# ScalarE writes the normalised tokens of the first pass, gain and bias go into the weights, inputs and statistics run a block ahead

## The reference

```
def _ln(x, g, b):
    m = jnp.mean(x, axis=-1, keepdims=True)
    v = jnp.mean(jnp.square(x - m), axis=-1, keepdims=True)
    return (x - m) * jax.lax.rsqrt(v + EPS) * g + b
h1 = _ln(x, n1_g, n1_b)
x = _attn(h1, h1, q1, k1, v1, o1_w, o1_b, heads) + x
h2 = _ln(x, n2_g, n2_b)
x = _attn(h2, context, q2, k2, v2, o2_w, o2_b, heads) + x
h3 = _ln(x, n3_g, n3_b)
proj = h3 @ ff_w1 + ff_b1
a, g = jnp.split(proj, 2, axis=-1)
return a * jax.nn.gelu(g, approximate=False) @ ff_w2 + ff_b2 + x
```

## Time and profile before

| | |
|---|---|
| median of 3 runs (lowest to highest) | 1429.01 us (1424.47 to 1432.35) |
| time of the profiled execution | 1427.96 us |
| its span, first to last instruction | 1426.1 us |
| mean granted TensorE clock | 0.966 |
| first pass | 0 to 156.1 us of the span |
| T0, T1, T2, T3, T7, end of PE's values | 20.87, 42.67, 57.41, 79.82, 140.54, 152.66 us |
| PE busy over the span | 93% |

### The profile page before, as it was taken

One profiled execution on the slowest core, in us unless ns is written; L12 is line 12 of the kernel. 1 busy time (PEld: TensorE's weight loads), 2 busy tenths in 40 slices (PEclk: granted clock), 3 DMA queues, 4 the chain that ended last, 5 costly groups with the idle time before them and its releaser, 6 DMA issues. The chain is left out here.

```text
span 1426.1 us, 35161 instructions
## 1 busy us (share of the span) xinstructions
PE 1321.4 (93%) x13343; PEld 1228.8 (86%) x13343; DVE 865.8 (61%) x1782; ACT 658.8 (46%) x1521; POOL 369.5 (26%) x468
## 2 busy tenths in 40 slices
PE   3899678999999999999999999999749999999999
PEld 3788667898989989988899899898539999999999
DVE  6776346777777777777777777776355424242421
ACT  2334125565655656656556565565334232323131
POOL 4211312222122122221221212212026342424241
PEclk9999689999999999999999999999759999999999
DMA  4667344444444554554544444442111000000000
GB/s 119 202 195 254 127 120 128 131 150 123 139 143 119 158 154 141 149 157 141 172 126 144 133 133 144 124 123 92 29 41 58 32 29 19 28 18 28 19 5 24
DMA packets 122663, 155.77 MB, mean 109 GB/s; under 512 B 25856, under 2 KB 116368, under 8 KB 122512
## 3 DMA queue, kind: packets, MB, share of 16 engines
q1 hardware_dynamic: 122512, 153.71, 35.4%
HBM read 63.24 MB, written 28.93 MB: 65 GB/s over the span
## 5 line engine op out<-in xcount | busy, mean ns | idle before, releaser
L661 DVE TENSOR_REDUCE neg_max<-score 100x2 f32<-100x722 f32 (+1 forms) x384 | 367.9, 958 | 158.9 <-PE score L499 76.5
L858 ACT ACTIVATE probs<-expin 120x400 f32<-120x400 f32 (+2 forms) x640 | 304.5, 502 | 169.1 <-PE expin L525 162.0
L525 PE MATMUL expin<-qs,ks 128*120 128x200 f32 (+2 forms) x1280 | 233.1, 282 | 10.8 <-DMA qs<-max_parts 7.9
L525 PEld LDWEIGHTS expin<-qs,ks 128*120 128x120 f32 (+2 forms) x1280 | 190.9, 184 | 33.3 <-issue 11.2
L499 PE MATMUL score<-ks,qs 128*100 128x362 f32 x640 | 169.6, 346 | 6.6 <-DVE neg_max L661 3.9
L1661 DVE SCALAR_TENSOR_TENSOR hidden<-ps_a,b_cols,gelu 128x320 f32<-128x320 f32 x100 | 55.1, 551 | 166.4 <-PE ps_a L1584 166.0
L1828 POOL TENSOR_TENSOR hid_lo<-hidden,hid_hi 128x320 fp32r<-128x320 f32 x100 | 88.1, 881 | 127.0 <-ACT hid_hi L1739 126.7
L928 POOL TENSOR_TENSOR var_eps<-mv,eps 100x1 f32<-100x1 f32 x32 | 6.1, 190 | 440.0 <-DVE mv L728 440.0
L1751 ACT ACTIVATE gelu<-ps_g,b_cols 128x320 f32<-128x320 f32 x100 | 52.8, 528 | 138.0 <-PE ps_g L1584 137.8
L546 PE MATMUL attn<-probs,vc 120*17 120x100 f32 (+1 forms) x3840 | 103.6, 253 | 0.0
L499 PEld LDWEIGHTS score<-ks,qs 128*100 128x100 f32 x640 | 82.7, 167 | 19.9 <-issue 14.0
(11 more groups left out here) (166 smaller groups left out, 2887.0 us busy)
## 6 DMA issues: line engine op xcount, KB each, us to landing
ks<-kc_parts SPq DMA_DIRECT2D x192, 181.0 KB, 2.7
qk_dram<-qk_parts SPq DMA_DIRECT2D x32, 500.0 KB, 4.9
qs<-q_parts SPq DMA_DIRECT2D x192, 75.0 KB
ks<-qk_dram SPq DMA_DIRECT2D x96, 125.0 KB
ctx_raw<-in_ctxT SPq DMA_DIRECT2D x64, 180.5 KB
ks<-kc_parts SPq DMA_DIRECT2D x96, 90.5 KB, 2.2
qs<-qk_dram SPq DMA_DIRECT2D x64, 125.0 KB
v_dram<-v_rows SPq DMA_DIRECT2D x32, 132.8 KB
```

The source lines that it names most:

```text
L525: mm = pe.matmul(dst, ks[a][u][:, c, j0:j0 + n], qs[a][u][:, :, q_slot(c) if a == 2 else c, :], start=True, stop=True)
L661: nc.vector.tensor_reduce(dst, src, AX_X, ALU.max, negate=True).then_inc(max_made, 1)
L858: nc.scalar.activation(probs[e % NPT][0:n, :], expin[e % 2][0:n, 0:HG * N], ACT.Exp, scale=SCALE)\
```

## The change

- **z on ScalarE.** DVE's two operations for a tile are gone. ACT writes z in one, `x * rstd + shift` with both factors per partition; POOL makes `shift` = -mean * rstd, so it has four operations for a tile in place of two.
- **Gain into the weights.** `qkv_high` and `qkv_low` multiply by the gain (a column per partition) while they split, with a sixth slot of `w_qkv` for the third that is used by the low parts. The bias goes through PE: `first_bias(y)` multiplies the spread bias with the raw weights, and `first_bias_high/low` put the split result into rows 64 to 127 of slot 5, against which `f_lo` has rows of ones. q2 is handled the same way, and `q2_gain` is gone.
- **Rows of factors.** Instead of gain and bias spread over 100 partitions, and of single columns of the second norm, four short rows are loaded ahead of x1; PE turns them (`turn_rows`) and DVE spreads them.
- **A block ahead.** Statistics are made for block k+2 in block k, x is loaded for block k+3, and z for tile b+2 is made behind the split of tile b.
- **Entry of the attention periods.** POOL no longer fills `ks[2]` there: most is cleared in the first pass, the two rows of ones come by two DMAs from a row set by POOL. DVE clears `attn` behind its first period instead of ahead of it.

```diff
             load_x(0)
-            rows(g_rows, given["n1_g"], landed["rows"])
-            rows(b_rows, given["n1_b"], landed["rows"])
-            load_x(1)
...
+            for a in (1, 2):
+                turned_rows(a)
+            for b in range(1, NB):
+                load_x(b)
+            for y in range(2):
+                weight(raw_qkv[:, y], given["qk"[y]], landed["qk"[y]])
+            for b in range(NB, NB + 2):
+                load_x(b)
+            weight(raw_qkv[:, 2], given["v"], landed["v"])
+            for b in range(NB + 2, 3 * NB):
                 load_x(b)
...
             for k in range(NK):
-                if k + 2 < NK:
-                    for b in range((k + 2) * NB, (k + 3) * NB):
+                if k + 3 < NK:
+                    for b in range((k + 3) * NB, (k + 4) * NB):
                         load_x(b)
                 if k == 0:
                     sp.wait_ge(w_lo_made, 3)
+                    sp.wait_ge(bias_full, 3)
...
+            def first_bias(y):
+
+                pe.wait_ge(landed["qkv"[y]], 48)
+                bias_of(1, BIAS[y][:, 0:D], raw_qkv[:, y]).then_inc(bias_full, 1)
...
             for k in range(NK):
                 for t in range(5):
                     queries_keys(k, t)
+                    if k == 0 and t == 1:
+                        first_bias(2)
                     if t < NB and k + 1 < NK:
                         turn_tile((k + 1) * NB + t)
...
-                link(nc.vector.scalar_tensor_tensor(out=centred[b % 2][:], in0=x[b % (2 * NB)][:], scalar=mv[:, i, 0:1], in1=g_rows[:],
-                                                    op0=ALU.subtract, op1=ALU.mult))
-                dve.wait_ge(rstd_made, b + 1)
-                nc.vector.scalar_tensor_tensor(out=z[b % 2][:].rearrange("p (k d) -> p k d", k=2), in0=twice(centred[b % 2][:]),
-                                               scalar=rstd[:, i:i + 1], in1=twice(b_rows[:]), op0=ALU.mult, op1=ALU.add)\
-                    .then_inc(z_made, 1)
...
                 for t in range(1, 5):
                     if k + 1 < NK:
-                        if t < 3:
-                            normalise(nxt + 1 + t)
                         features_low(nxt + t - 1)
+                    if k + 2 < NK:
+                        normalise(after + t - 1)
                     queries_keys_low(k, t)
...
+            def scale(b):
+                i = b % NX
+                act.wait_ge(rstd_made, b + 1)
+                if b > 1:
+                    act.wait_ge(turned, b - 1)
+                nc.scalar.activation(z[b % 2][:].rearrange("p (k d) -> p k d", k=2), twice(x[b % NX][:]), ACT.Identity,
+                                     bias=shift[:, i:i + 1], scale=rstd[:, i:i + 1]).then_inc(z_made, 1)
+
             def qkv_high(y):
...
+                for i, k, n in ((0, 0, P), (1, 2, P), (4, 1, P), (5, 1, 64)):
+                    ins = nc.scalar.activation(in_order(w_qkv[:, i], y)[0:n], as_read(raw_qkv[:, y, k, :], y)[0:n], ACT.Copy,
+                                               scale=gain[1][0:n, k:k + 1])
                 ins.then_inc(w_hi_made, 1)
...
+            act.wait_ge(cols_read, 1)
+            qkv_high(0)
+            qkv_high(1)
+            for y in range(2):
+                first_bias_high(y)
+            qkv_high(2)
+            for b in range(NB, NB + 2):
+                scale(b)
...
                     if t < NB and k + 1 < NK:
-                        features_high((k + 1) * NB + t)
+                        features_high(nxt + t)
+                        if nxt + t + 2 < B:
+                            scale(nxt + t + 2)
...
                 link(nc.gpsimd.tensor_tensor(var_eps[:, i:i + 1], mv[:, i, 1:2], eps[0:N, :], ALU.add))
-                nc.gpsimd.tensor_tensor(rstd[:, i:i + 1], var_eps[:, i:i + 1], neg_half[0:N, :], ALU.pow)\
+                nc.gpsimd.tensor_tensor(neg_mean[:, i:i + 1], mv[:, i, 0:1], neg_one[0:N, :], ALU.mult)
+                link(nc.gpsimd.tensor_tensor(rstd[:, i:i + 1], var_eps[:, i:i + 1], neg_half[0:N, :], ALU.pow))
+                nc.gpsimd.tensor_tensor(shift[:, i:i + 1], neg_mean[:, i:i + 1], rstd[:, i:i + 1], ALU.mult)\
                     .then_inc(rstd_made, 1)
...
+            period(*roles(PERIODS[0]))
+            nc.vector.memset(attn[:, :], 0.0).then_inc(attn_cleared, 1)
             for u in range(2):
                 nc.vector.memset(neg_max[2][u][:], 0.0)
             nc.vector.memset(q2_rows[:], 0.0)
-            nc.vector.memset(attn[:, :], 0.0).then_inc(attn_cleared, 1)
-            for p in PERIODS:
+            for p in PERIODS[1:]:
                 period(*roles(p))
```

More of the change, by code:

```diff
@@ L371, in period @@
                 store_x2(x)
+            sp.wait_ge(ones_made, 1)
+            ones = pv[2][0:2, 0:JP]
+            for u in range(2):
+                sp.dma_start(ks[2][u][0:P:64].bitcast(F32), ones.unsqueeze(1).broadcast_to([2, HP, JP])).then_inc(keys_set, 16)
             for p in PERIODS:
@@ L494, in cross_scores @@
                     pe.wait_ge(kc_landed[c // 4][u], 16 * 3 * (b // 2 + 1))
+                if b == 0 and c == 0:
+                    pe.wait_ge(keys_set, 32)
                 if c == 0:
@@ L955, in _ @@
             pool.sem_inc(ones_set, 1)
-            for u in range(2):
-                link(nc.gpsimd.memset(ks[2][u][:].bitcast(F32), 1.0))
-            pool.sem_inc(keys_set, 1)
             for p in PERIODS:
@@ L1106, in turn_tile, with turn_rows @@
                 mm.then_inc(turned, 1)
+            def turn_rows():
+                pe.wait_ge(landed["rows"], 64)
+                for j in range(3):
+                    mm = pe.transpose(qk_ps[0][:, 4 * j:4 * j + 4], rows[:, j * P:(j + 1) * P], identf[0:4, 0:4])
+                mm.then_inc(cols_full, 1)
             def empty(m):
@@ L1138, in _ @@
             pe.wait_ge(ident_step, 2)
+            turn_rows()
             for b in range(NB):
                 turn_tile(b)
+            pe.wait_ge(cols_read, 1)
+            for y in range(2):
+                first_bias(y)
             pe.wait_ge(w_lo_made, 2)
+            pe.wait_ge(bias_lo_made, 2)
             for k in range(NK):
@@ L1148, in _ @@
                     pe.wait_ge(w_lo_made, 3)
+                    pe.wait_ge(bias_lo_made, 3)
                 if k == 2:
@@ L1254, in _ @@
             nc.vector.memset(one[:], 1.0).then_inc(one_set, 1)
-            for b in range(NB):
+            normalise(0)
+            spread_columns()
+            for b in range(1, NB):
                 normalise(b)
-            dve.wait_ge(landed["rows"], 32)
             dve.wait_ge(ones_set, 1)
             for b in range(NB):
-                scale(b)
-            for b in range(NB):
                 features_low(b)
-            for y in range(3):
+            for y in range(2):
                 qkv_low(y)
+            for y in range(2):
+                first_bias_low(y)
             for b in (NB, NB + 1):
                 normalise(b)
-                scale(b)
-            second_bias_cols()
+            qkv_low(2)
+            for b in (NB + 2, NB + 3):
+                normalise(b)
+            spread_second_bias()
             for k in range(NK):
-                nxt = (k + 1) * NB
+                nxt, after = (k + 1) * NB, (k + 2) * NB
                 queries_keys_low(k, 0)
@@ L1331, in q2_high @@
             def q2_high():
-                act.wait_ge(q2_scaled, 1)
-                nc.scalar.copy(w_q2[:, 0:2, :], raw_q2[:, 0:3:2, :])
-                nc.scalar.copy(w_q2[:, 4, :], raw_q2[:, 1, :])
-                nc.scalar.copy(w_q2[0:64, 5, :], raw_q2[0:64, 1, :]).then_inc(q2_hi_made, 1)
+                act.wait_ge(landed["q2"], 48)
+                for i, k, n in ((0, 0, P), (1, 2, P), (4, 1, P), (5, 1, 64)):
+                    ins = nc.scalar.activation(w_q2[0:n, i, :], raw_q2[0:n, k, :], ACT.Copy, scale=gain[2][0:n, k:k + 1])
+                ins.then_inc(q2_hi_made, 1)
             def second_bias_high():
@@ L1416, in _ @@
             link(nc.gpsimd.memset(t_lo["T2"][64:P, 1, :].bitcast(F32), 1.0))
-            for b in range(NB + len(clear), B):
+            for b in range(NB + 2 + len(clear), B):
                 inverse_deviation(b)
```

215 lines of the change are left out of this document (119 added, 96 removed).

## The result

The changed kernel takes 1410.92 us, median of 5 runs (1409.4 to 1416.37); the kernel before, run beside it, 1424.58 (1421.97 to 1432.35, 5 runs). The ratio is 0.9897, with a 95% interval of 0.9861 to 0.9933: 1.0% faster, 13.7 us between the medians. The profiled execution took 1412.06 us with a span of 1409.93, where that of before had 1426.12.

The account below looks back on a forecast made before the run. DVE was taken to set the first pass's pace, with PE the bound after the change. From 1427.96 us, -1.3 + 0.5 - 7.0 - 7.7 - 0.5 = -16.0 gave 1412.0 us, range 1408 to 1416.

Parts of the forecast that it names:

- The bound and the steady blocks: First pass, blocks 3 to 6: PE becomes the bound, 13.25 us a block, 53.0 in place of 60.72: -7.7 us.
- The price of z: One z on ACT: 0.48 us for 384 columns, 0.67 by the skill's rule; slot with bank and tile 1.4 us.
- Block 1: First pass: ACT's first copy of values waits for a late store, PE 2.0 us (up to 3.6): +0.5 us.
- rival 2: The DMA queue becomes the bound, blocks of 14.3 us in the first pass: -10.7 in all, 1417.3 us; chance 0.16.
- Block 2: First pass: x loaded earlier, context-split stall of 1.0, bias product 1.2: 15.45 us for 22.41, -7.0.
- Start: Up to T1: T0 at 20.2 us (19 to 21.5), T1 at 41.3 for 42.67: -1.3.
- Entry: Start of the attention periods: clearing off the path -1.1 us, context's load behind two DMAs +0.6: -0.5.
- The base: The sum started from the profiled execution of the kernel before, 1427.96 us, taken as 1 us under the median.
- Rival 4: Slower: stores landing over 10 us after issue hold ACT's bank copy, z and PE's transposes: 1436 us; chance 0.04.

Follow-up runs that it names:

- e5: The changed kernel with z made on VectorE again, by one operation on x: 1420.22 us, ratio 0.9964 to the kernel before.
- e6: The changed kernel with each tile's statistics made in the block that uses them, not a block ahead: 1416.24 us, ratio 0.9930 to the kernel before.
- e4: The changed kernel with each weight's middle third loaded by two DMAs of 64 rows in place of one: 1404.61 us, ratio 0.9865 to the kernel before.
- e14: e13 with the context's and o1's weights loaded and split a block later: 1407.87 us, ratio 0.9886 to the kernel before.
- e11: e4 with POOL's fills of v_rows and bias_cols behind the fourth tile's deviation, not the second's: 1403.49 us, ratio 0.9855 to the kernel before.
- e13: e11 with statistics of tiles 4 and 5 ahead of VectorE's weight splits and POOL's stack fills in larger pieces: 1403.54 us, ratio 0.9857.

## Why the prediction was right, and where its terms were not

- **The bound and the steady blocks**: right. 13.25 a block forecast, 13.06 to 13.40 measured; DVE at 6.9 us a block (27.42 / 4) for 6.7; no waits for z there. Of the three parts of the change e5 shows that one operation less is nearly enough to free VectorE in these blocks (busy for 32.28 of 53.27 us, 0.56 us longer than with the change), and e6 that the statistics' lead is worth 3.3 us. What z on ScalarE brought in the first pass lies for the greater part at the start, where it keeps z clear of POOL's fills. The prediction had credited it with the steady blocks.
- **The price of z**: the value from rows, 0.48, was wrong; it is 0.715. The estimate from the Trainium skill's rule ("ScalarE: Activation LUTs", What ACT_TABLE_LOAD costs), 0.67, came closer. The slot is 1.4 us even so, as forecast, but by luck: the sum left out that the three operations overlap, by about as much as z was too cheap. It stays inside 1.74, so the miss cost nothing.
- **Block 1**: this is the term of the sum that was mis-sized most. "I take 2.0, nearer the upper end of the landing but not at it" was 4.94. The prediction had the place, the first copy of values in block 1, the mechanism, a store behind weights in the queue, and a bound of 3.6, which rested on stores that land no later than 55.3. They landed at 55.6 (0.3 later), PE wanted its bank at 51.2 (0.5 sooner), and the copy itself, 0.5 with its hand-over, had not been counted: 1.3 in all. Behind the stall the clock fell, which the sum had put only into a rival; 16 matmuls took 4.12 us there and 2.50 ahead of it, which is 1.6 of the other 1.8 of 19.79 - 13.06. The rule on two engines stood in the prediction beside rival 2 and was not used here, where it sets the landing: e4, which removes just that, removes all of +5.05 and 1.7 more.
- **Block 2**: -6.15 for -7.0. The stall of 0.93 us for the context's split is the 1.0 of the sum, and e14 shows that it moves with the split. The 0.8 that are missing are the bias product's. Its six matmuls cost 1.90 us, from 69.66 to 71.56, and not 1.2: the sum took the 1.9 of before for the price at half speed, but it was that of the full clock already, as the stretch of that product in the kernel before shows, with a granted clock of 1.00:

```profile
73.30:75.20 1.90, 1.90 (x7) 0.86 (x6) 1.13 (x4) 0.49 (x1) 0.00 (x0) 1.00 0.00 0
```

  That the greater part of the gain comes from the earlier load of x rests on the traces: DVE's wait of 2.50 us for x has no counterpart in the block now. No run undoes that load alone.
- **Start**: T0 at 20.2 was wrong by 2.2 us, and outside its own 19 to 21.5. The sum counted ACT's and DVE's extra splits, but not that PE's own two bias products stand between the fourth transpose and the first group (13.35 to 21.3, at the slow pace); e4 and e11 show that this chain, not the landing, sets T0. In return the full pace came a group sooner, which is luck by e13 and e14: T1 was 1.2 us ahead of the forecast.
- **Entry**: -1.1 for the wait is right, and the DMA fill costs about 1 ahead of `expin`, for +0.6. The -4.7 in place of it is the clock, 0.84 for 0.79; unchanged code had 0.79 and 0.82. The prediction left the clock out of this stretch.
- **The base**: the profiled execution of before was 1427.96, 3.4 us above the median of the kernel before as it ran beside the changed one. A sum of -16.0 from 1424.6 would have been 1408.6; the measured difference of medians is 13.7. That the forecast of 1412.0 was only 1.1 off is luck: the base was too high, block 1 too short, and the entry's clock made up for it.
- **Rivals**: rival 2's blocks of 14.3 did not come (DMA share 0.78, 13.2 us). Rival 4's threshold, a landing of 10 us after the issue, was passed once, in block 1: 10.4 from the start of the four issues (45.24 to 55.63). What ACT's wait stopped there was the copy of a bank and with it PE's values; no transpose waited for a z behind it.

## What to carry to other kernels

Before a load is moved ahead or beside stores, look for stretches of a microsecond in which the DMA share is 0.13 to 0.14: here such transfers held up what was issued behind them, and splitting them along partitions was worth 6.3 us, nearly half as much as the whole rewrite. When work is taken from a full engine, try the smaller step (one operation in place of two) and the larger (another engine) apart: here the smaller was nearly enough for the steady blocks, and the larger paid at the start, where fills of another engine ran beside it. Where two profiles differ in a stretch, look first whether the instruction counts are equal and the granted clock is not; a stretch that PE enters from idle moved by 4 us with unchanged code. And set a sum against its parts: this one came out right with two parts wrong by about 5 us each.

## What the runs showed of the hardware that was not expected

- A `TENSOR_SCALAR` of 100x384 takes VectorE 0.47 to 0.48 us; six that began during a fill of POOL's took 0.74 to 2.40 us and ended 0.20 to 0.22 us behind it (e5).
- ScalarE's activation with scale and bias both read per partition: 0.715 us for 384 columns; a cast of 400 takes 0.488. Bank, tile and z one behind another take 1.41 us together, 0.2 less than the sum of the three.
- From the first scores on the same 617 matmuls take PE 65.68 to 75.79 us at granted clocks of 0.86 to 0.74 of full speed (2.4 GHz), with the whole stretch longer by as much.
- A float32 pair of 320 columns takes 1.27 to 1.44 us at the half pace and 0.70 to 0.80 at the full one.
- While a 64-row third goes to both halves of the partitions by one DMA, the queue moves 47 to 49 GB/s with a share of 0.13 to 0.14.
